# GpSimd's waits before the row gathers of a four-layer graph kernel: at the product's signal, and a further wait at each fourth group

## What is computed

```python
x = x + _L0_gnn_ref(_layernorm(x), edge_index, edge_weight, ...)   # two graph layers with weighted norms, relu, a product
x = x + _L0_ffn_ref(_layernorm(x)[None], ...)[0]                   # 8 experts, the same 2 for all rows
x = x + _L1_gnn_ref(_layernorm(x), ..., edge_index)                # two graph layers with norms from the degrees
x = x + _L1_ffn_ref(_layernorm(x)[None], ...)[0]                   # 8 experts, one for each row, with a capacity
```

## Time and profile before

| what | value |
|---|---|
| runs of the kernel before | median 4722.83 us, 4721.35 to 4726.13, 3 runs |
| profiled execution | span 5647.3 us from the first to the last instruction; no time of its own is given beside the span |
| TensorE busy | 4017.9 us, 71% of the span |
| VectorE busy | 3072.1 us, 54% |
| GpSimd busy | 2967.7 us, 53% |
| granted TensorE clock, mean over the span | 0.835 |

### The profile page before, as it was taken

One profiled execution on the slowest core, in us unless ns is written; L12 is line 12 of the kernel. 1 busy time (PEld: TensorE's weight loads), 2 busy tenths in 40 slices (PEclk: granted clock), 3 DMA queues, 4 the chain that ended last, 5 costly groups with the idle time before them and its releaser, 6 DMA issues.

```text
span 5647.3 us, 64923 instructions
## 1 busy us (share of the span) xinstructions
PE 4017.9 (71%) x21108; PEld 3177.4 (56%) x21109; DVE 3072.1 (54%) x7978; ACT 1485.5 (26%) x4028; POOL 2967.7 (53%) x3232
## 2 busy tenths in 40 slices
PE   7764555555546676777778977788776778785999
PEld 6653433334335466666666755666655666664766
DVE  7765645555447655555555565555546554443434
ACT  6502322232232222222223322222231111124221
POOL 7736466666656555555640016555556555543233
PEclk9987777776678777777779988899988998997999
DMA  2423433333333222222221013333333332225231
GB/s 89 122 68 93 118 96 97 96 96 96 97 89 87 78 80 79 80 80 80 82 67 34 20 60 87 89 92 90 90 102 97 102 93 84 83 77 176 69 104 54
DMA packets 272106, 489.99 MB, mean 87 GB/s; under 512 B 85684, under 2 KB 176805, under 8 KB 271635
## 3 DMA queue, kind: packets, MB, share of 16 engines
q0 software_dynamic: 139312, 377.94, 23.8%
q1 hardware_dynamic: 125336, 101.03, 5.9%
q10 hardware_dynamic: 7118, 6.83, 0.4%
HBM read 426.41 MB, written 62.17 MB: 87 GB/s over the span
## 4 chain that ended last, share of the span: by engine, by line
PE 39%; another core or an unknown queue 23%; DVE 22%; issue 10%; ACT 3%; DVEq 2%; POOL 1%; DMA 1%; ACTq 0%; SPq 0%; POOLq 0%
PE PSA L1020 11%; PE PSA L1164 5%; DVE ACC L2016 4%; PE PSA L1411 4%; PE PSA L1397 4%; PE PSA L1173 3%; PE PSA L1298 3%; PE PSA L1314 3%; DVE XIN L1989 2%; DVE XT L1989 2%; PE PSA L985 1%; PE PSA L979 1%; DVE WORK L2282 1%; PE PSA L1149 1%
## 5 line engine op out<-in xcount | busy, mean ns | idle before, releaser
L853 POOL DMA_INDIRECT WORK<-tab,SRC x2632 | 2522.8, 958 | 2146.8 <-issue 768.0
L2016 DVE TENSOR_TENSOR ACC<-ACC,PSA 64x256 f32 x1360 | 568.9, 418 | 1457.7 <-remote 959.4
L1020 PE MATMUL PSA<-WORK,XIN 128*128 128x256 f32 x3192 | 960.0, 454 | 458.0 <-ACT XIN L1491 341.5
L1020 PEld LDWEIGHTS PSA<-WORK,XIN 128*128 128x128 f32 x3192 | 711.0, 233 | 612.1 <-issue 492.5
L1020 PE MATMUL PSA<-WORK,XT 128*128 128x256 f32 x2072 | 594.5, 437 | 161.4 <-ACT XT L1491 85.4
L1020 PEld LDWEIGHTS PSA<-WORK,XT 128*128 128x128 f32 x2072 | 439.4, 222 | 248.9 <-issue 172.6
L1149 PE MATMUL PSA<-WORK 128*128 128x256 bf16 x784 | 161.6, 290 | 327.4 <-DVE WORK L2282 98.2
L1173 PE MATMUL PSA<-WORK,XT 128*128 128x42 f32 x832 | 153.8, 350 | 211.8 <-DVE WORK L1989 211.7
L1149 PEld LDWEIGHTS PSA<-WORK 128*128 128x128 bf16 x784 | 69.4, 104 | 379.8 <-issue 230.4
L1989 DVE TENSOR_TENSOR XIN<-PSA,DST 128x512 f32<-128x512 f32 x412 | 279.1, 679 | 2.5 <-DVE PSA L2323 1.4
L1173 PEld LDWEIGHTS PSA<-WORK,XT 128*128 128x128 f32 x832 | 145.8, 260 | 223.7 <-DVE WORK L1989 221.7
(11 more groups left out here) (492 smaller groups left out, 6899.0 us busy)
## 6 DMA issues: line engine op xcount, KB each, us to landing
WORK<-tab,SRC POOLq DMA_INDIRECT x2632
ACC<-in_L_ffn_w SPq DMA_DIRECT2D x16, 1024.0 KB
tab<-WORK SPq DMA_DIRECT2D x98, 128.0 KB
slots_x<-FILL SPq DMA_DIRECT2D x4, 2080.0 KB
ACC<-slots_x SPq DMA_DIRECT2D x8, 910.0 KB
tab<-ACC SPq DMA_DIRECT2D x49, 128.0 KB
WORK<-tab SPq DMA_DIRECT2D x49, 128.0 KB
before_y<-X SPq DMA_DIRECT2D x7, 896.0 KB
```

What stands on the lines that cost most here:

```text
L853: po.indirect_dma_start(out=rows[:, 0:width], out_offset=None, in_=tab[:, :], in_offset=bass.IndirectOffsetOnAxis(ap=SRC[:, c:c + 1].bitca ...
L1020: last = pe.matmul(PS[h][:, 0:D], chosen[:, j * P:(j + 1) * P], rows[:, 0:D], start=(j == 0), stop=(j == Q - 1))
L2016: return ve.tensor_tensor(rows, rows, PS[h][half, 0:D], ALU.add)
```

## The change

GpSimd's wait before a group changes its semaphore: in place of s_free (the group that held the place has been added to the sums) it is s_p (its product is done). Only the first five groups of layer 2 keep s_free. And in layers 1 to 3 each group g that is divisible by four, from 8 on, also waits until s_p is at BEGIN + g - 1, thus until the products of the layer's groups up to g - 2 are done.

```diff
@@ -838,13 +838,17 @@
             def gather_edges(layer, tab, width):
                 for g in range(GROUPS_OF[layer]):
                     m = turn_of(layer, g)
-                    if layer >= 2:
-                        po.wait_ge(s_free, 4 + BEGIN[2] + max(0, BEGIN[layer] - BEGIN[2] + g - RK + 1))
+                    if layer == 2 and g < RK:
+                        po.wait_ge(s_free, 4 + BEGIN[2])
+                    elif layer >= 2:
+                        po.wait_ge(s_p, BEGIN[layer] + g - RK + 1)
                     elif in_x(layer, g):
                         if g >= ROUND:
-                            po.wait_ge(s_free, 4 + g - ROUND + 1)
+                            po.wait_ge(s_p, g - ROUND + 1)
                     elif m >= RS_:
-                        po.wait_ge(s_free, 4 + group_of_turn(m - RS_) + 1)
+                        po.wait_ge(s_p, group_of_turn(m - RS_) + 1)
+                    if layer and g % 4 == 0 and g >= 8:
+                        po.wait_ge(s_p, BEGIN[layer] + g - 1)
                     if layer == 0 and 2 <= g < ROUND:
                         po.wait_ge(s_dp, RS_ * (g - 1))
                     landed = (s_rx if in_x(layer, g) else s_row)[slot_of(layer, g)]
```

## The result

| kernel | median us | runs | ratio to before |
|---|---|---|---|
| before | 4724.48 | 4 (4721.35 to 4728.42) | |
| after | 4798.44 | 4 (4781.78 to 4811.25) | 1.0150 (1.0136 to 1.0164) |

The change makes the kernel 74 us slower. The profiled execution of after took 4781.78 us, the shortest of its four runs, with a span of 4780.1 us. The profiled execution of before spans 867 us more and cannot be laid beside it, so before was profiled once more.

What follows compares the result with a forecast made beforehand. GpSimd's gather issue bounds the kernel: 1390 + 3305 + 5 + 20 = 4720 us against a median of 4722.8. Waits of 22.4 less 1.2 for places give +21 us, 4744 us, range 4698 to 4800.

Steps and rivals of the forecast that it cites:

- GpSimd sets the pace: Whole kernel: GpSimd issues gathers nearly without a break, 5.0 us a group, and what delays it is paid in full.
- the places: Places free at the product's signal instead of the add: 1.2 us gained at layer 0's start, 0 elsewhere.
- I take 0.2 us for each, 22 us: Layers 1 to 3: cost of the 112 fourth-group waits on GpSimd, 0.2 us each, 22 us in all.
- the upper bound of 62: Most the 112 waits should cost: 0.55 us each, the mean overshoot of four groups at the openings, 62 us.
- The openings: Starts of layers 2 and 3, where four groups' products were read ending 5.6, 7.2, 4.2 and 4.3 us behind their gathers.
- The allowance: At each fourth-group wait: it costs nothing if g - 2's product ends within 5.3 us of its last gather.
- the holds: In the trace, long unbroken gather runs hold up TensorE until they end; the runs have 35 us of them at most.
- the 925 us: Whole kernel before: the profiled span of 5647.3 us over the runs' median of 4722.8, put down to stalls in the trace.
- No change: Rival, chance 0.28: the 5.3 us allowed hold in nearly all groups, 0.05 us a wait, +4 us, 4727 us.
- Faster: Rival, chance 0.18: in layers 1 to 3, pauses shorten small stalls of TensorE present in the runs too, 4700 us.
- Much slower: Rival, chance 0.09: TensorE runs dry at each wait and GpSimd waits a full 1 us, 112 us, 4835 us.
- The sign that the prediction named for this rival: Profile after, ahead of groups 8, 12, 16: GpSimd pauses of 3 us and more without a hold would mean much slower.

Runs made afterwards that it cites:

- again: The kernel before, unchanged, profiled once more: 4729.97 us, span 4728.3 us.
- after_b: The kernel after, unchanged, run once more on another chip: 4795.36 us, 1.0146 of before there.
- waits_only: Before with only the wait of each fourth group added, places still freed at the add: 4808.12 us, 1.0168 of before.
- only1: After with the fourth-group waits in layer 1 alone: 4762.21 us, 1.0069 of before.
- only23: After with the fourth-group waits in layers 2 and 3 alone: 4756.48 us, 1.0052 of before.
- every2_b: After with the wait at each second group from 8 on in place of each fourth, 224 waits: 4830.12 us, 1.0226 of before.
- tight_b: After with the fourth-group wait up to the product of g - 1 in place of g - 2: 5354.31 us, 1.1332 of before.
- late_start: After with the fourth-group waits from group 16 on in place of 8: 4782.32 us, 1.0115 of before.
- loose: After with the fourth-group wait up to the product of g - 3 in place of g - 2: 4732.71 us, 1.0012 of before.

## Why the prediction was right or wrong

**Right: GpSimd sets the pace, and a delay of it is paid in full.** 4720 us was worked out from 661 groups of 5.0 us; `again` shows GpSimd without a pause in the three layers, and what its pauses add is nearly what the span adds: 51 and 51.8 us (after), 65 and 67.8 (after_b), 74 and 80.6 (waits_only), 27.5 and 24.8 (only1), 24.5 and 27.8 (only23), 85 and 90.5 (every2_b), 620 and 617 (tight_b: 718.4 us of waiting, less 52.9 and 151 x 0.3). It is 10 us off in the two others, 40 and 50.7 (late_start), 4 and -6.3 (loose). That the sum came within 3 us of the median was luck in part. In `again` the gathers of the 661 groups take 3342 us in place of 3305, layer 1's 5.13 us a group, and all else 1386 us in place of 1415, since the stretches were read from the longer execution.

**Right: the places.** 1.1 us were gained where 1.2 was forecast, and nothing elsewhere, since GpSimd never waits for a place in `again` after the first.

**Wrong: "I take 0.2 us for each, 22 us".** This is the step that failed, a term of the right kind and the wrong size. The 112 waits cost 50.7 us in the profiled execution (0.45 each) and 74 us in the medians (0.66), which is above the upper bound of 62 as well. That 4798.44 still lies within the whole range, up to 4800, is luck: its upper end was drawn halfway to the rival in which TensorE runs dry at each wait, and that is not what happened. Four things lie in the wrong size.

*The openings were read too short.* Groups 1 to 3 stood for all. The first wait is at group 8 and hangs on group 6, and from group 5 on the products are late, behind VectorE and the units. In `again` group 6 of layer 2 has:

```profile
2849.26 0.95 POOL L853 DMA_INDIRECT WORK<-tab,SRC  x1 [0.30 <-issue]
...
2865.35 1.89 PE L1020 MATMUL PSA<-WORK,XIN 128*128 128x256 f32 x8
```

From 2850.21 to 2867.24 are 17.0 us, and 16.5 in layer 3. These two places alone made 22.5 us in after, as much as was forecast for all 112.

*The clock in layer 1.* A product of 1.9 us takes 3.6 at the lower level (the one at 1914.15 below, granted 0.56), and 74 of the 208 products in layer 1 of `again` take over 2.5 us (80 in after). At the waits the median one of these ends 5.4 us behind its last gather. In after, 13 of the 20 waits of layer 1 that cost something hang on one, 19.2 of their 26.9 us. The prediction took the product "at speed" from the earlier trace rows, though the earlier trace rows had a clock of 0.75 for layer 1.

*The allowance was 0.8 us too wide.* The product had until the start of g's first gather, 5.3 us. But a gather that really waits starts 0.76 us after the product's end: so in layer 2 above (2893.67 to 2894.43), and in layer 1 from 1917.71 to 1918.48:

```profile
1914.15 3.56 PE L1024 MATMUL PSA<-WORK,XIN 128*128 128x256 f32 x8
...
1918.48 0.94 POOL L857 DMA_INDIRECT WORK<-tab,SRC  x1 [3.76 <-PE PSA L1024]
```

So a wait is free only up to 5.3 - 0.76 = 4.5 us. With this, the pause is the product's end + 0.76 less the end of group g - 1's last gather + 0.30, where that is positive. Worked out for all 112 waits of after it gives 26.4, 10.7 and 13.6 us, and measured are 26.9, 10.8 and 13.7. On `again`, where no pause gives TensorE time to catch up, the same sum gives 33, 33 and 39 us: a bound from above of 106 us that such a trace of before would have given. The loss in the medians, 74, lies between that and the 51 of one execution.

*One execution isn't the median.* The profiled run is the shortest of the four. The rest of the 74 us is in runs of which no trace was kept; that they hold more pauses of the same kind, as after_b and waits_only do (65 and 74 us), is inferred.

**Wrong: what the holds are.** The prediction took the 925 us as something that exists in the trace alone, and named the rule of the Trainium skill, "NOTIFIC — the notification-queue block", section 7.1, in support. On chip C the traced execution and the others agree to 0.1%, and none of the eleven traces from chips A, B and D has a wait for "remote", nor has that of after. So tracing alone doesn't make them: where there are holds, they are the chip's, or of something on it. Whether the block that the page describes ever holds back its producers, no run here shows; it was no ground for taking a traced stall as an effect of the trace. The conclusion drawn from it, that the runs of before have no holds, was true all the same, by luck, because their median is that of chips like A; the profiled execution of before looks like one on a chip like C (5647.3 us against 5617.40). That is argued from the likeness, and no record here says on which chip it ran.

**The rivals.** *No change* put 0.05 us on a wait; loose is the kernel for which it would have been true. *Faster* needed holds in the runs, and on chip C they are there, but after loses 12% there and only the wait at each second group gains. Whether that gain is its mechanism, holds ended sooner, no run shows. *Much slower* had TensorE running dry each time and a full 1 us per wait. In layers 2 and 3 of after one and two waits of 31 cost anything. The sign that the prediction named for this rival, pauses of 3 us and more without a hold, did show, but at four places only (3.5, 4.3, 10.7 and 11.9 us). Where TensorE does run dry, in tight_b, it is 5.6 us per wait.

## What to carry to other kernels

When one engine sets the pace, price an added wait by the whole distribution of lags at the groups it hangs on, the openings of stages and the products at the low clock among them, and not by the typical group: the mean of the overshoot counts, and the typical group's is zero. A wait that leaves one group of slack costs 1.5% here, with two groups 0.1%, with none 13%, on chips without holds; so ask for the slack in microseconds against the longest lags before asking what the wait is good for. And when a profiled execution is far from the runs, profile again on another chip before explaining the difference.

## What the runs showed of the hardware

- On chip C TensorE issues single matmuls 0.7 to 1.4 us apart while GpSimd's gathers run, and before takes 5617 us; on three other chips 4725 to 4730. The expert stage without gathers takes 390.9 us on both kinds.
- A gather of 32 rows holds GpSimd for 0.86 us, one of 128 rows for 0.95, and 0.30 us lie between two in either case.
- A gather that waits for a product starts 0.75 to 0.78 us after the product's modelled end in all 22 such waits of after's trace, where a gather without a wait follows the one before it after 0.30.
- A product takes 1.9 us at the granted clock's upper level and 3.6 to 3.8 at the lower. In tight_b, with pauses of 5 to 7 us at each fourth group, layer 2's granted clock was 0.88 in place of 0.97, and the first product behind 110 of the 112 waits was a slow one. Of the products that the waits hang on, 18 of 112 were slow, against 23 of the same ones in after.
